# Last attention, second sequence: the products of value sums with reciprocals that were read back, on VectorE in place of GpSimd

## The reference

```python
xn = _layernorm(x)
s  = attention(xn)
g  = _silu(ffn(xn))
x  = x + s * g
```

```python
q = (x @ Wq).reshape(b, n, HEADS, DIM_HEAD).transpose(0, 2, 1, 3) * scale
kv = x @ Wkv
kv = jnp.concatenate([jnp.broadcast_to(null_kv, (b, 1, DIM_HEAD)), kv], axis=1)
sim = jnp.einsum('bhid,bjd->bhij', q, kv)      # then the causal mask
attn = jax.nn.softmax(sim.astype(jnp.float32), axis=-1)
out = jnp.einsum('bhij,bjd->bhid', attn, kv.astype(jnp.float32))
return out.transpose(0, 2, 1, 3).reshape(b, n, HEADS * DIM_HEAD) @ Wout
```

## Time and profile before

| | us |
|---|---|
| three runs: median (lowest to highest) | 1989.89 (1984.07 to 1990.84) |
| profiled execution: span from its first to its last instruction | 1987.3 |
| busy in the span: TensorE, VectorE, ScalarE, GpSimd | 1839.8, 1337.9, 963.6, 1239.5 |

### The profile page before, as it was taken

One profiled execution on the slowest core, in us unless ns is written; L12 is line 12 of the kernel. 1 busy time (PEld: TensorE's weight loads), 2 busy tenths in 40 slices (PEclk: granted clock), 3 DMA queues, 4 the chain that ended last, 5 costly groups with the idle time before them and its releaser, 6 DMA issues.

```text
span 1987.3 us, 31683 instructions
## 1 busy us (share of the span) xinstructions
PE 1839.8 (93%) x9960; PEld 1273.0 (64%) x9960; DVE 1337.9 (67%) x3765; ACT 963.6 (48%) x2008; POOL 1239.5 (62%) x1454
## 2 busy tenths in 40 slices
PE   5999999999895899999999999999889999998985
PEld 4566666666595566676766567887556666555564
DVE  8888888888344767666666546556776777764533
ACT  2534445445455455554555534545344545444543
POOL 1767789889654467767777710011367888799953
PEclk8999999999998899999999999999799999999997
DMA  5224243232153443443444220000313223223243
GB/s 150 67 61 116 64 107 91 63 78 61 53 175 85 95 95 82 109 95 90 102 93 100 66 88 22 1 13 1 85 44 71 63 69 77 69 67 86 63 122 101
DMA packets 138508, 155.95 MB, mean 78 GB/s; under 512 B 34420, under 2 KB 78740, under 8 KB 138084
## 3 DMA queue, kind: packets, MB, share of 16 engines
q1 hardware_dynamic: 134244, 145.80, 30.0%
q0 software_dynamic: 4096, 8.12, 1.2%
HBM read 47.96 MB, written 17.52 MB: 33 GB/s over the span
## 4 chain that ended last, share of the span: by engine, by line
PE 62%; DVE 12%; POOL 11%; issue 6%; DMA 3%; ACT 3%; SPq 2%; POOLq 0%; DVEq 0%; ACTq 0%
PE P L904 61%; POOL acc L1701 4%; POOL yd L1724 3%; DVE mx L2112 2%; DMA qA<-hq 2%; POOL acc L1698 1%; SPq L1828 1%; DVE P L2123 1%; POOL xg L1715 1%; POOL pr L1679 1%; PE P L1003 1%; ACT pr L1444 1%; PE P L942 0%; DMA xl<-yd 0%; POOL z L1707 0%
## 5 line engine op out<-in xcount | busy, mean ns | idle before, releaser
L1701 POOL TENSOR_TENSOR acc<-acc,pr 128x512 f32<-128x512 f32 (+5 forms) x640 | 660.3, 1051 | 47.2 <-ACT pr L1444 22.5
L1444 ACT ACTIVATE pr<-P 128x512 f32<-128x512 f32 (+1 forms) x768 | 396.7, 568 | 321.4 <-PE P L904 278.8
L904 PE MATMUL P<-pr,vt 128*64 128x512 f32 (+3 forms) x2304 | 402.7, 490 | 4.9 <-POOL pr L1679 4.9
L904 PE MATMUL P<-qA,kA 128*128 128x512 f32 (+2 forms) x1024 | 389.2, 383 | 12.5 <-ACT pr L1444 11.6
L904 PE MATMUL P<-qB,kB 128*128 128x512 f32 (+2 forms) x1024 | 367.7, 365 | 0.0
L904 PE MATMUL P<-kA,qA 128*128 128x512 f32 (+2 forms) x1152 | 314.8, 376 | 32.0 <-DMA qA<-hq 12.3
L1679 POOL TENSOR_SCALAR_AFFINE_SELECT pr<-pr 128x256 f32<-128x256 f32 x384 | 157.3, 411 | 275.6 <-ACT pr L1444 214.6
L904 PEld LDWEIGHTS P<-pr,vt 128*64 128x64 f32 x2304 | 154.0, 137 | 225.7 <-issue 191.1
L2112 DVE TENSOR_REDUCE mx<-P 128x1 f32<-128x512 f32 x384 | 243.4, 683 | 40.2 <-PE P L904 37.9
L904 PEld LDWEIGHTS P<-qA,kA 128*128 128x128 f32 x1024 | 195.1, 191 | 95.7 <-ACT pr L1444 46.6
L904 PEld LDWEIGHTS P<-kA,qA 128*128 128x128 f32 x1152 | 194.5, 197 | 94.7 <-issue 25.0
(11 more groups left out here) (355 smaller groups left out, 2847.4 us busy)
## 6 DMA issues: line engine op xcount, KB each, us to landing
qA<-hq SPq DMA_DIRECT2D x384, 128.0 KB
kA<-stage SPq DMA_DIRECT2D x158, 128.0 KB
qB<-qB SPq DMA_DIRECT2D x96, 128.0 KB, 2.3
kB<-stage SPq DMA_DIRECT2D x79, 128.0 KB
rb<-sum_share SPq DMA_DIRECT2D x60, 128.0 KB
yd<-in_c_zero SPq DMA_DIRECT2D x32, 128.0 KB, 2.7
w<-in_L_W SPq DMA_DIRECT2D x16, 256.0 KB
xg<-xg SPq DMA_DIRECT2D x24, 129.0 KB
```

The costliest lines, as they stand in the source:

```text
L904: return P.matmul(out, lhs, rhs, start=start, stop=stop)
L1444: S.activation(a.pr[slot][:, r, 512 - wide:512], m.bank[b][:, 512 - wide:512], AF.Exp, scale=0.125).then_inc(s.free[b], 1)
L1701: G.tensor_tensor(acc[:, :, sl], acc[:, :, sl], pt[:, :, sl], ALU.add).then_inc(s.acc, 1)
```

## The change

In the second sequence (b = 1) the products `div` of pairs 0 to 6, both chunks, fourteen in all, are done by VectorE in place of GpSimd, at the same place of the order and with the same waits. They count on a semaphore of their own, `div_v`. To make room, the two semaphores `t_in` are given up, and the loads that used them count on `f2_in`, so that all who wait for `f2_in` or did for `t_in` now wait for five loads.

In `signals` and `Plan`:

```diff
-    s.f_in, s.u_in, s.t_in, s.a2_in, s.a2w_in, s.h_in = one("f_in"), some("u_in", 2), some("t_in", 2), one("a2_in"), some("a2w_in", 3), one("h_in")
+    s.f_in, s.u_in, s.div_v, s.a2_in, s.a2w_in, s.h_in = one("f_in"), some("u_in", 2), one("div_v"), one("a2_in"), some("a2w_in", 3), one("h_in")
...
-                self.n_div[it[1:]] = len(self.n_div) + 1
+                self.n_div[it[1:]] = len([x for x in self.n_div if x[1] == it[2]]) + 1
...
-            return self.s.div, self.n_div[L, b, p, c]
+            return self.s.div_v if b else self.s.div, self.n_div[L, b, p, c]
```

In the programs of TensorE (the third layer's last projection), ScalarE (`f2sp`, `f2g`), GpSimd, SP (`f2ld`) and VectorE, in this order:

```diff
-                w.wait_ge(s.f2_in, 16 * 3)
+                w.wait_ge(s.f2_in, 16 * 5)
...
-                w.wait_ge(s.t_in[k[0]], 16)
+                w.wait_ge(s.f2_in, 16 * 5)
...
-                w.wait_ge(s.f2_in, 16 * 3)
+                w.wait_ge(s.f2_in, 16 * 5)
...
-            elif kind == "div" and not at_once(*k[0:3]):
+            elif kind == "div" and not at_once(*k[0:3]) and not k[1]:
...
-                    Y.dma_start(f.tmp[0][:], d["L2_w1"]).then_inc(s.t_in[0], 16)
-                    Y.dma_start(f.tmp[1][:], d["L2_w2"]).then_inc(s.t_in[1], 16)
+                    Y.dma_start(f.tmp[0][:], d["L2_w1"]).then_inc(s.f2_in, 16)
+                    Y.dma_start(f.tmp[1][:], d["L2_w2"]).then_inc(s.f2_in, 16)
...
+            elif kind == "div" and not at_once(*k[0:3]) and k[1]:
+                a, n = m.A[k[0]], pl.cast_slot(m.A[k[0]], *k)[0]
+                z = a.z[pl.chunk(*k) % 4]
+                w.wait_ge(*pl.emptied("pv", *k, 0))
+                w.wait_ge(s.cast, 32 * od.nth("cast", *k))
+                V.tensor_tensor(z[:], z[:], a.rb[n][:], ALU.mult).then_inc(s.div_v, 1)
```

## The result

The changed kernel takes 2004.74 us (median of 4 runs, 1999.25 to 2010.13), the kernel before 1988.74 beside it. The ratio is 1.008 with a 95% interval of [1.0061, 1.01]: 16 us slower, where 1983.9 had been forecast and 1994 was the end of the range. The profiled execution of after has a span of 2004.8 us, before 1987.3.

What follows compares the result with a forecast made beforehand. The prediction took GpSimd to set the pace from 1742 us on. It summed 8.3 us saved on GpSimd less 2.3 us for an early VectorE hold to 6.0 us, giving 1983.9 us against the 1989.9 median, range 1976.5 to 1994.

Steps and rivals of the forecast that it cites:

- GpSimd's relief: Second sequence, mainly after 1742 us: products leaving GpSimd, 1.23 us each less 0.33 for the port, save 8.3 us.
- The early hold: Ahead of 1742 us, second chunk's product: VectorE stands for read-back and a sum, delaying row maxima; cost 2.3 us.
- The port: At each moved product: VectorE stands until GpSimd's instruction ends, then GpSimd loses 0.33 us, leaving 0.90 us per product.
- reaches GpSimd mostly with 5 us of lead: In GpSimd's stretch from 1742 us: what waits for VectorE has this cover, so its holds there cost 0.
- The last two fall into idle spells of VectorE: Last two moved products, near the end: VectorE is idle there, one spell 9.83 us long, so their holds cost 0.
- the fourth: Head pairs from the first chunks on: VectorE's holds become the pace, 35.1 us per pair, 14 us slower, 2004; chance 0.12.
- GpSimd idle for ScalarE in the stretch: Among the scatters after 1742 us: GpSimd idle before sums would show the forecast wrong; no size given.
- the 3.24 us in which TensorE waits for GpSimd anyway: Near the scatter of 1775.38 us: TensorE's existing wait, 3.24 us, taken as evidence against VectorE's holds becoming the pace.

Runs made afterwards that it cites:

- e6: Changed kernel, but VectorE takes a row maximum of the value sums in place of each product, without waiting for the read-back (division left out): 1978.52 us.
- e3: Changed kernel with only the seven products of chunk 0 on VectorE, those of chunk 1 back on GpSimd: 1988.79 us, 0.999 of the kernel before.
- e5: Changed kernel, but VectorE's products multiply by a constant tile and do not wait for the read-back (reciprocals left out): 1985.74 us.
- e8: Changed kernel with VectorE's chunk 1 product moved ahead of the router's row numbers: 2005.98 us, 1.0089 of the kernel before.
- e2: Changed kernel with only the seven products of chunk 1 on VectorE, those of chunk 0 back on GpSimd: 2009.18 us, 1.009 of the kernel before.
- e10: Changed kernel, but GpSimd's 1024-wide sum ahead of each chunk 1 product waits until VectorE's product is done: 1985.45 us, 0.9985 of the kernel before.
- e4: Changed kernel, read-back wait kept, but VectorE takes a row maximum of the reciprocals in place of each product (division left out): 1989.26 us.
- e9b: Changed kernel with the chunk 1 product later, behind the next chunk's reciprocals, on VectorE; a repeat timing: 1982.33 us, 0.9973 of the kernel before.
- e9: Changed kernel with the chunk 1 product later, behind the next chunk's reciprocals, on VectorE; first timing: 1981.5 us, 0.9972 of the kernel before.

## Why the prediction was wrong

- **GpSimd's relief, 8.3 us:** right in kind and near in size. Without the 0.33 us for the port the same sum is 8 x 1.23 + 0.2 + 1.23 = 11.3 us, and e6, without port and wait, measures 10.1 in the time and 7.6 in the changed stretch. Fourteen products left its program (its line has 16 in after), and it stopped being the pace.
- **The early hold, 2.3 us:** right. The forecast let the second product end at 1714.8; it ran from 1713.33 to 1715.0, and the first scatter is 2.9 us late. In e3, without chunk 1 on VectorE, it is 0.8 us late, counted from GpSimd's last product of the first sequence.
- **The port:** the step "VectorE stands until GpSimd's instruction ends, and that GpSimd then loses about 0.33 us" was right, and GpSimd's share nearly so: the scatter behind a held product takes 1.26 us (1784.54), beside 0.99. But this share is the small one. VectorE's own, 2.2 to 2.9 us over the 0.69, was not in the sum at all in this stretch. By the rule that I had cited (the Trainium skill, SBUF — State Buffer, "Who interferes with whom": whoever comes first has the port) VectorE would have been through, since by the profile it started 0.49 us ahead of the sum; the trace shows it standing nevertheless. Nothing above depends on that rule.
- **The step that failed is "reaches GpSimd mostly with 5 us of lead"**, in the paragraph on what is given to VectorE. I costed the holds in GpSimd's stretch at nothing by that lead. I checked it for what leads GpSimd, not for what stands between VectorE and GpSimd: TensorE's banks. For the product of 1711.97 I had named this very chain, maxima, banks, matmuls, priced it at 2.3 us, and then not repeated it for the chunk 1 products that have the same place in every later pair. The four of them among the scatters take 3.2 us in the mean, behind a wait of 0 to 1.5, and use up the lead within a pair; from then on GpSimd waits for exponentials (21.4 us in 12 waits, before 5.7 in 3).
- **"The last two fall into idle spells of VectorE":** right; they took 0.69 and 0.72 us. But the third from last, the first behind the last scatter (1886.92), was left at nothing by the same lead. The chain that ended last runs through it: the read-back's transfers of 4.10 us (1882.73), the product of 1.39 us, which a sum holds, the first maximum, and TensorE, which waits 3.4 us for it. 7.1 us of the loss lie behind the last scatter. e3, with no chunk 1 product on VectorE, loses 1.1 us there (39.9 from last scatter to last sum, before 38.8).
- **The rivals:** the fourth had the mechanism, the place and the size: 35.1 us per pair (34.5 and 35.4 measured), 2004 us (2004.74). It charged both chunks, though, with 3.2 of its 6.0 us for chunk 0, which costs nothing (e3), so that its number came out so near is in part luck. The sign that it had named, GpSimd idle for ScalarE in the stretch, is there. It had 0.12, against a speaking row, "the 3.24 us in which TensorE waits for GpSimd anyway". That is cover of one wait in a pair for two holds, and it stands at another place of the pair than the maxima.

A row of the kernel before would have warned me. Its groups on VectorE by shape (1560 to 1900 us; busy us, mean ns), and the timeline of one such instruction beside GpSimd's:

```profile
L2133 DVE TENSOR_TENSOR mx<-mx,sn 128x8 fp32r<-128x8 f32 x22 | 18.8, 853 | 0.7
```
```profile
1752.61 1.76 DVE L2134 TENSOR_TENSOR mx<-sn,mx 128x8 f32<-128x8 f32 x1
```
```profile
1752.50 1.85 POOL L1701 TENSOR_TENSOR acc<-acc,pr 128x768 f32<-128x768 f32 x1
```

An instruction on 8 columns with a mean of 853 ns is not working but standing, for the sums: the one shown, of the next line and the same shape, ends at 1754.37, the sum at 1754.35. It shows from the very stretch how long VectorE stands, where I had taken the port's price from another layer.

What stays open: why a product that began up to 0.69 us ahead of a sum, beside a scatter, is still caught by that sum (seen eight times in after, e5 and e8, and three times in e2), while three of e5's that began 0.14 us ahead of a sum, beside a mask, were done in 0.68 us. That the one began ahead of the other is known from the profile's starts alone. And what the wait alone costs beside e6, 8.6 us by the medians and 2.8 in the changed stretch, is not traced to its instructions.

## What to carry to other kernels

When an instruction moves to an engine that is not the bottleneck, price not only its duration but what it will be made to stand for there, and follow what is queued behind it through every engine until something has slack; a queue that was priced once at one place must be priced again at each repeat of that place. Look for small instructions with long mean times: they tell what standing at a shared port costs, and who pays. If two engines must meet, let the one with the short instruction go first, by a wait on the other or by another place in the order (here 0.34 us of waiting in place of 2.7 us, or a place behind the urgent work). Look first at what that instruction waits for itself: behind the last scatter e10 made GpSimd stand 3.53 us for a read-back.

## What the hardware showed that I had not expected

- The port is paid unevenly. Across a 2.35 us sum the product of 0.69 us takes 2.9 to 3.6 us and ends 0.55 or 0.56 us behind the sum, each of four times; the sum is not lengthened, and only the scatter behind it is, by 0.27 us.
- Two costs of 8.6 and 8.0 us make 26.1 us together (e4, e5, after against e6; in the changed stretch 2.8 and 10.0 make 25.2), because the one mostly brings about the meeting in which the other is paid.
- TensorE's clock was low behind its idle time. Behind the idle 4.58 us of after, four matmuls took 1.98 us, in the earlier trace rows 1.08. The granted clock was 0.51 there, the level of 1.2 GHz (the row below, columns as in the earlier trace rows), and 1.00 at the four of the earlier trace rows (1712.8 to 1714 us). In e10, behind a wait of 1.45 us, it was 0.50 as well (1833.9 to 1836), so e10 does not win this back everywhere. The granted clock of the stretch was 0.94 in after, 0.96 before and 1.00 in e9b, so part of the loss and of e9's gain is clock, between the levels of 1.2 and 2.4 GHz; how much of it, no run here tells apart.

```profile
1785.60:1787.70 2.10, 2.02 (x6) 0.44 (x6) 1.79 (x4) 0.01 (x1) 2.00 (x3) 0.51 0.10 31
```
